# Exchanging the engines of two PSUM evacuations in a windowed-attention loop

## The chip, the cores and the metric

The kernel runs on all 8 cores of one Trainium2 chip. Each core works on its own 2048 of the 16384 tokens and reads all weights; no core waits for another. The metric is the device time of the slowest core, in microseconds. A core has five engines with queues of their own that run in order: TensorE (PE), VectorE (DVE), ScalarE (ACT), GpSimd (POOL) and SyncE (SP). They meet only at semaphores.

## The reference

One transformer layer on x of 2 x 8192 tokens with 1024 features, in 16 heads of 64:

```python
x = x + attn(_layernorm(x), Wq, Wk, Wv, Wo)
x = x + moe(_layernorm(x), gate_w, gate_b, w1, b1, w2, b2)

# attn: windows of 128 tokens, and the sequence's first 64 tokens as global keys
s_g = einsum('bhnqd,bhgd->bhnqg', qw, kg) * scale      # 64 global keys
s_l = einsum('bhnqd,bhnkd->bhnqk', qw, kw) * scale     # 128 keys of the window
attn = softmax(concatenate([s_g, s_l], axis=-1), axis=-1)
out = einsum(attn[..., :g], vg) + einsum(attn[..., g:], vw);  return out @ Wo.T
# moe: all 8 experts, (silu(gh + b) * (xh + b)) @ w2, weighted by a top-2 gate
```

## The kernel before

The program is written by hand: a helper `op(engine, function, waits, inc)` appends to one list per engine, and `runner` (L871) issues each list in order. Before every instruction of ACT or DVE, `runner` also makes the engine wait for its own previous counted instruction (L877). Counters `c_pe`, `c_act`, `c_dve` each stand for one semaphore that is raised by every counted instruction of that engine, so a value of a counter names a place in that engine's list; a wait whose value was already waited for is left out (L880).

Stages, in order: load x and normalize it (LayerNorm by ACT squares and DVE sums); then twice, for each half of 1024 tokens, transpose the normalized tokens, project to q, k, v (`projection`, L302, into PSUM banks pE and pF, evacuated by ACT), and run the attention loop of L519; then the second LayerNorm with the gate; then the experts from L739 on, which are all dense matmuls on PE with weights streamed by POOL's DMA queue.

The change is in the attention loop. A **pair** `pi` is one window (8 per half) with one head (16), so 128 pairs per half. A pair goes through four steps, and the loop at L519 is a software pipeline written out by hand: in **round** j it emits, in this order,

- now and then (j = 22, 38, ...: 8 times per half) `pemit_oproj`, the output projection of a finished window: 2 groups of 8 matmuls of 512 columns, each group added to x by DVE (L506), and then a square-sum of the new x by ACT (L512) and a sum by DVE (L516);
- `pemit_pv(j-6)`: PE multiplies the transposed probabilities `sPT` with the values (L467 for the global keys, L474 for the window) into bank pC or pD, 64 x 128; the result is copied from PSUM to `aof` by DVE (L478);
- `pemit_tr(j-5)`: PE transposes the probabilities `P_sb` in two parts (L447, L452) into pT or pU; they are copied from PSUM to `sPT`, 128 x 256 in bf16, by ACT (L455);
- `pemit_front(j-3)`: ACT takes the exponential of the scores with the row sum as accumulator (L430, two instructions in the trace); DVE takes the reciprocal (L435) and scales the row (L438);
- `pemit_S(j)`: PE computes the scores in two matmuls (L417, L422) into one of three banks pA, pB, pE, after the exponential of pair j-3 has left that bank: `vEXP.get(pi - 3)` in L414.

`sPT` has 2 slots, `P_sb` 4, and pC/pD and pT/pU are each two banks used in turn.

Of the kernel before, what the change touches and what calls it, by code (L numbers as in the profile page):

```python
# [8 lines left out]
BF16 = mybir.dt.bfloat16  # L9
# [4 lines left out]
P = 128  # L14
# [5 lines left out]
HD = 64  # L20
NWIN = 16
GT = 64
# [23 lines left out]
def build_nc(taps=()):  # L46
    nc = bass.Bass("TRN2", target_bir_lowering=False)
# [58 lines left out]
    c_pe = Ctr(sem_pe)  # L106
    c_act = Ctr(sem_act)
    c_dve = Ctr(sem_dve)
# [9 lines left out]
    def op(eng, fn, waits=(), inc=None):  # L118
        streams[eng].append((fn, tuple((c, v) for (c, v) in waits), inc))
        if inc is not None:  # L120
            inc.v += inc.step
        return inc.v if inc is not None else None

    xr = d_x.rearrange("(t p) d -> p t d", p=P)
    for ch in range(4):
        op("sync" if ch % 2 == 0 else "scalar", lambda e, ch=ch: e.dma_start(
            out=x_sb[:, ch * 4:(ch + 1) * 4, :], in_=xr[:, ch * 4:(ch + 1) * 4, :]),
           inc=c_x[ch])
# [76 lines left out]
    def norm_transpose(tt, dst_view, v_extra_waits=(), src=None, parts=P,  # L205
# [30 lines left out]
    es_attn = contextlib.ExitStack()  # L236
# [9 lines left out]
    vgt = es_attn.enter_context(nc.sbuf_tensor("vgt", [GT, D], BF16))  # L246
    gx = es_attn.enter_context(nc.sbuf_tensor("gx", [GT, 8], F32))
    P_sb = es_attn.enter_context(nc.sbuf_tensor("P_sb", [P, 4, 192], BF16))
    sPT = es_attn.enter_context(nc.sbuf_tensor("sPT", [P, 2, 256], BF16))
    rr = es_attn.enter_context(nc.sbuf_tensor("rr", [P, 4, 4], F32))  # L250

    op("sync", lambda e: e.dma_start(out=xg_sb[:], in_=d_xg), inc=c_sy)
# [4 lines left out]
       waits=[(c_sy, v_sync_all[0]), (c_setup, v_gpsetup)], inc=c_dve)  # L257
    op("vector", lambda e: e.tensor_tensor(s_gbl[:], s_gbf[:], s_gbh[:], ALU.subtract),
       inc=c_dve)
# [6 lines left out]
       waits=[(c_sy, v_sync_all[0])], inc=c_act)  # L266
    op("vector", lambda e: e.reduce_sum(gx[:, 0:1], xg_sb[:], axis=AX.X),
       waits=[(c_sy, v_sync_all[0])], inc=c_dve)
    v_gxs = (c_act.v, c_dve.v)
    op("vector", lambda e: e.tensor_scalar_mul(gx[:, 2:3], gx[:, 0:1], 1.0 / D),  # L270
       waits=[(c_act, v_gxs[0])], inc=c_dve)
# [6 lines left out]
       waits=[(c_dve, v_gv)], inc=c_act)  # L278
    op("scalar", lambda e: e.activation(gx[:, 4:5], gx[:, 4:5], AF.Exp, scale=-0.5),
       inc=c_act)  # L280
# [3 lines left out]
       waits=[(c_act, v_grstd)], inc=c_dve)  # L284
# [9 lines left out]
    v_aof_done = [0]  # L294
    v_attn_tail_pe = [0]

    def wproj_load(slot, dram, vfree_pe):
        op("gpsimd", lambda e: e.dma_start(out=wsl[:, slot], in_=dram),
           waits=([(c_pe, vfree_pe)] if vfree_pe else []), inc=c_wsl[slot])
        return (c_wsl[slot], c_wsl[slot].v)  # L300
# [33 lines left out]
    for half in range(2):  # L334
        hbase = half * 8
        v_xn1 = 0
        for t8 in range(8):
            tt = hbase + t8
            waits = [(c_act, v_ln1_rstd), (c_dve, v_ln1_nmr)]
# [14 lines left out]
        if half == 0:  # L354
            for ic in range(DC):
                ps = proj_ps[ic % 2]
                waits = [vwk, (c_act, v_xgn)]
# [3 lines left out]
                for dc in range(DC):  # L361
                    def f(e, ps=ps, dc=dc, ic=ic):
# [5 lines left out]
                       inc=(c_pe if dc == DC - 1 else None))  # L368
# [6 lines left out]
        v_v_act, v_v_pe = projection(vt, 0, vwv, half, 1.0, v_xn1, "tm")  # L375
        if half == 0:
            for tc in range(2):
                ps = proj_ps[tc % 2]
                waits = [vwv, (c_act, v_xgn)]
# [3 lines left out]
                for dc in range(DC):  # L383
                    def f(e, ps=ps, dc=dc, tc=tc):
# [4 lines left out]
                       inc=(c_pe if dc == DC - 1 else None))  # L389
# [3 lines left out]
                   waits=[(c_pe, v_mm)], inc=c_act)  # L393
                v_evac_prev[("proj", tc % 2)] = c_act.v
        vwo = wproj_load(1, d_wot, v_k_pe)
# [6 lines left out]
        vPN = {}  # L402
        vPT = {}
        vPTEV = {}
        vPV = {}
        vAO = {}
# [36 lines left out]
        def pemit_tr(pi):  # L443
            ptb = pT if pi % 2 == 0 else pU

            def ft1(e, ptb=ptb, pi=pi):
                return e.transpose(ptb[0:GT, 0:P], P_sb[:, pi % 4, 0:GT], s_id[:])  # L447
            op("tensor", ft1,
               waits=[(c_dve, vPN[pi]), (c_act, vPTEV.get(pi - 2, 0))], inc=None)

            def ft2(e, ptb=ptb, pi=pi):
                return e.transpose(ptb[:, P:256], P_sb[:, pi % 4, GT:192], s_id[:])  # L452
            op("tensor", ft2, inc=c_pe)
            vPT[pi] = c_pe.v
            op("scalar", lambda e, ptb=ptb, pi=pi: e.copy(  # L455
                sPT[:, pi % 2, :], ptb[:, 0:256]),
               waits=[(c_pe, vPT[pi]), (c_pe, vPV.get(pi - 2, 0))], inc=c_act)
            vPTEV[pi] = c_act.v

        def pemit_pv(pi):  # L460
            w8, head = pi // H, pi % H
            pvb = PV_banks[pi % 2]
            pb = (head % 2) * HD
            ic = head // 2

            def fpv1(e, pvb=pvb, head=head, pi=pi):
                return e.matmul(pvb[0:HD, 0:P], vgt[:, head * HD:(head + 1) * HD],  # L467
                                sPT[0:GT, pi % 2, 0:P], start=True, stop=False)
            op("tensor", fpv1,
               waits=[(c_act, vPTEV[pi]), (c_act, v_v_act),  # L470
                      (c_dve, vAO.get(pi - 2, 0))], inc=None)

            def fpv2(e, pvb=pvb, head=head, w8=w8, pi=pi):
                return e.matmul(pvb[0:HD, 0:P], vt[:, w8, head * HD:(head + 1) * HD],  # L474
                                sPT[:, pi % 2, P:256], start=False, stop=True)
            op("tensor", fpv2, inc=c_pe)
            vPV[pi] = c_pe.v
            op("vector", lambda e, pvb=pvb, pb=pb, ic=ic, w8=w8: e.tensor_copy(  # L478
                aof[pb:pb + HD, ic, w8 * P:(w8 + 1) * P], pvb[0:HD, 0:P]),
               waits=[(c_pe, vPV[pi])], inc=c_dve)  # L480
            vAO[pi] = c_dve.v

        def pemit_oproj(t8):
            v_ao_w = vAO[t8 * H + H - 1]
            for dh in range(2):
                gidx = t8 * 2 + dh
                ps = pF
                waits = [vwo, (c_dve, v_ao_w)]
                pv = v_evac_prev.get("oproj1")
                if pv:  # L490
                    waits.append((c_dve, pv))
                pv2 = v_evac_prev.get(("proj", 1))
                if pv2:
                    waits.append((c_act, pv2))
                for ic in range(DC):
                    def f(e, ps=ps, ic=ic, t8=t8, dh=dh):
                        return e.matmul(ps[:], aof[:, ic, t8 * P:(t8 + 1) * P],  # L497
                                        wsl[:, 1, ic, dh * 512:(dh + 1) * 512],
                                        start=(ic == 0), stop=(ic == DC - 1))
                    op("tensor", f, waits=waits if ic == 0 else [],  # L500
                       inc=(c_pe if ic == DC - 1 else None))
                v_mm = c_pe.v

                def fr(e, ps=ps, t8=t8, dh=dh, hbase=hbase):
                    xs = x_sb[:, hbase + t8, dh * 512:(dh + 1) * 512]
                    return e.tensor_tensor(xs, ps[:], xs, ALU.add)  # L506
                op("vector", fr, waits=[(c_pe, v_mm)], inc=c_dve)
                v_evac_prev["oproj1"] = c_dve.v
                if dh == 1:
                    tt = hbase + t8  # L510
                    v_add = c_dve.v
                    op("scalar", lambda e, tt=tt: e.activation(  # L512
                        lnsq[:, 0:D], x_sb[:, tt, :], AF.Square,
                        accum_out=g_s2[:, tt:tt + 1]),
                       waits=[(c_dve, v_add)], inc=c_act)
                    op("vector", lambda e, tt=tt: e.reduce_sum(  # L516
                        g_s1[:, tt:tt + 1], x_sb[:, tt, :], axis=AX.X), inc=c_dve)

        for j in range(NPAIR + 24):  # L519
# [8 lines left out]
                pemit_front(j - 3)  # L528
            if j < NPAIR:
                pemit_S(j)  # L530
        v_aof_done[0] = c_dve.v

        v_attn_tail_pe[0] = c_pe.v
    v_attn_done_dve = c_dve.v
# [14 lines left out]
       waits=[(c_act, v_st[0])], inc=c_dve)  # L549
# [6 lines left out]
       waits=[(c_dve, v_var)], inc=c_act)  # L556
    op("scalar", lambda e: e.activation(g_rstd[:], g_rstd[:], AF.Exp, scale=-0.5),
       inc=c_act)
# [3 lines left out]
       waits=[(c_act, v_rstd2)], inc=c_dve)  # L562
# [108 lines left out]
    for j in range(NT + 2):  # L671
# [9 lines left out]
       waits=[(c_pe, v_attn_done_pe)], inc=c_setup)  # L681
# [57 lines left out]
    for ei in range(NE):  # L739
        for jfi in range(NJ):  # L740
            for fsl in range(FS_JF):
                fs = jfi * FS_JF + fsl
                slot = (ei * NFS + fs) % W1SLOTS
                for th in range(NTH):
                    par = g1[0] % 2
                    xh, gh = xh_b[par], gh_b[par]
                    waits = [w1_fill_v[(ei, fs)],
                             (c_act, v_ln2_done_act),
                             (c_dve, v_gate_done_dve)]
# [7 lines left out]
                    for hx in range(2):  # L757
                        ps = xh if hx == 0 else gh
                        for dc in range(DC):
                            def f(e, ps=ps, slot=slot, dc=dc, hx=hx, th=th):  # L760
# [5 lines left out]
                               waits=waits if (hx == 0 and dc == 0) else [],  # L766
                               inc=(c_pe if (hx == 1 and dc == DC - 1) else None))
                    v_mm = c_pe.v
                    if th == NTH - 1:
# [5 lines left out]
                       waits=[(c_pe, v_mm), (c_act, v_b1_done)], inc=c_act)  # L775
                    v_a1 = c_act.v

                    def fa2(e, xh=xh, par=par, ei=ei, fs=fs, fsl=fsl, th=th):
# [5 lines left out]
                       inc=c_dve)  # L784
# [3 lines left out]
            for tt in range(NT):  # L788
                for dh in range(2):
                    gq = (tt * 2 + dh) % 2  # L790
                    ps = m2_b[gq]
                    waits = [(c_dve, v_act_ready),
                             (c_dve, v_gate_done_dve),
                             (c_setup, v_b2ld)]
# [6 lines left out]
                    if jfi == 0:  # L801
# [7 lines left out]
                        waits = []  # L809
                    for fsl in range(FS_JF):  # L810
# [3 lines left out]
                        def f(e, ps=ps, fsl=fsl, slot=slot, tt=tt, dh=dh,  # L814
# [6 lines left out]
                           inc=(c_pe if fsl == FS_JF - 1 else None))  # L821
                        first = False
                        waits = []
# [18 lines left out]
    for tt in range(NT):  # L842
        op("sync", lambda e, tt=tt: e.dma_start(
            out=out_r[:, tt, :], in_=x_sb[:, tt, :]),
           waits=[(c_dve, store_after[(tt, 1)])], inc=c_sy)
# [9 lines left out]
    for name in taps:  # L855
        t, dt_, shp = tapmap[name]
        dtap = nc.dram_tensor("tap_" + name, shp, F32, kind="ExternalOutput").ap()
        if dt_ == F32:
            op("sync", lambda e, t=t, dtap=dtap: e.dma_start(out=dtap, in_=t[:]),
               waits=[(c_dve, c_dve.v), (c_act, c_act.v), (c_pe, c_pe.v)], inc=c_sy)  # L860
        else:
            op("gpsimd", lambda e, t=t, dtap=dtap: e.dma_start(out=dtap, in_=t[:]),
               waits=[(c_dve, c_dve.v), (c_act, c_act.v), (c_pe, c_pe.v)], inc=c_setup)
# [77 lines left out]
```

How the kernel before makes its waits and increments, by code:

```python
            def body(eng):  # L872
                marks = {}
                own = own_ctr.get(name)
                n_own = 0
                for fn, waits, inc in streams[name]:
                    if own is not None and n_own > 0:
                        eng.wait_ge(own.sem, n_own)
                    for (ctr, v) in waits:
                        if v > marks.get(ctr.key, 0):
                            eng.wait_ge(ctr.sem, v)
                            marks[ctr.key] = v
                    ins = fn(eng)
                    if inc is not None:
                        assert ins is not None
                        ins.then_inc(inc.sem, inc.step)
                        if inc is own:
                            n_own += 1
```

## Time and profile before

| what | us |
|---|---|
| two plain runs | 6828.25 and 7522.56 |
| their median | 7175.41 |
| the profiled execution, slowest core | 6743.82 |
| its span, first to last instruction (core 2) | 6742.0 |
| spans of the 8 cores in it | 6729.4 to 6742.0 |

The two plain runs are of one program and lie 10% apart, and the profiled execution is lower than either. Durations can be read only from the profiled execution, so everything below is set against its 6743.8 us. Times in the rows are microseconds from the start of the span of core 2 unless they are marked ns. PE is the matmul part of TensorE, PEld its weight loads, which overlap with it. PEclk is the TensorE clock that was granted, as a share of 2.4 GHz: 1.00 is 2.4 GHz and 0.50 is 1.2 GHz.

### The profile page before, as it was taken

What the parts mean: (1) busy time and instruction counts of PE and PEld (TensorE: products, weight loads), DVE (VectorE), ACT (ScalarE), POOL (GpSimd) and SP (SyncE); (2) the same over time, 40 slices, a digit from 0 to 9 for tenths busy, and PEclk for the clock granted to TensorE, in tenths of its full rate; (3) what the DMA queues carried; (4) which work ended last, traced back from release to release, by engine and by line L of the source; (5) the groups of instructions that cost most, each with busy time, mean ns of one, the idle gap of its engine ahead of it and who ended that gap; (6) DMA issues with size and microseconds to landing.
All of it is one profiled execution on the core that took longest, in us unless ns stands there. A gap on an engine that the chain in (4) does not pass through costs nothing.

```text
span 6742.0 us, 77157 instructions; the slowest of 8 cores (6729.4 to 6742.0 us)
## 1 busy us (share of the span) xinstructions
PE 6071.4 (90%) x28296; PEld 2705.8 (40%) x28296; DVE 1859.3 (28%) x3088; ACT 1103.0 (16%) x2056; POOL 278.8 (4%) x530
## 2 busy tenths in 40 slices
PE   4557554999999999999999999999999999999999
PEld 2223223444444444444444444444444444444444
DVE  1231333222222222222222222222222222222222
ACT  3333333111111111111111111111111111111111
POOL 0000000000000000000000000000000000000000
PEclk9657555999999999999999999999999999999999
DMA  4002001122222222222222221222222222221122
GB/s 97 7 1 50 1 1 32 26 36 37 38 38 38 38 38 38 38 38 38 38 35 38 38 38 32 38 38 38 35 35 38 38 35 38 37 36 34 34 35 68
DMA packets 80461, 240.33 MB, mean 36 GB/s; under 512 B 9330, under 2 KB 9346, under 8 KB 79074
## 3 DMA queue, kind: packets, MB, share of 16 engines
q0 software_dynamic: 75312, 218.33, 19.4%
q1 hardware_dynamic: 3730, 12.88, 0.5%
q8 instruction: 238, 3.90, 0.2%
q10 hardware_dynamic: 1056, 4.19, 0.2%
q14 instruction: 125, 1.02, 0.0%
HBM read 445.29 MB, written 8.39 MB: 67 GB/s over the span
## 4 chain that ended last, share of the span: by engine, by line
PE 89%; ACT 5%; issue 2%; DVE 2%; another core or an unknown queue 1%; DMA 0%; ACTq 0%; DVEq 0%; POOLq 0%
PE pE L816 14%; PE pF L816 13%; PE pA L761 13%; PE pB L761 13%; PE pD L761 13%; PE pC L761 13%; ACT P_sb L430 2%; ACT sPT L455 1%; PE pF L497 1%; PE pE L314 1%; PE pF L314 1%; PE pE L803 1%; PE pF L803 1%; PE pD L474 0%
## 5 line engine op out<-in xcount | busy, mean ns | idle before, releaser
L816 PE MATMUL pE<-w2rg,act_sb 128*128 128x512 bf16 x4096 | 999.7, 389 | 65.9 <-DVE act_sb L779 35.1
L761 PE MATMUL pA<-xn2f,w1rg 128*128 128x512 bf16 x4096 | 969.3, 380 | 34.3 <-DVE x_sb L828 31.1
L816 PE MATMUL pF<-w2rg,act_sb 128*128 128x512 bf16 x4096 | 975.9, 382 | 0.0
L761 PE MATMUL pB<-xn2f,w1rg 128*128 128x512 bf16 x4096 | 968.7, 380 | 0.0
L761 PE MATMUL pC<-xn2f,w1rg 128*128 128x512 bf16 x4096 | 967.7, 379 | 0.0
L761 PE MATMUL pD<-xn2f,w1rg 128*128 128x512 bf16 x4096 | 967.7, 379 | 0.0
L772 ACT ACTIVATE a1st<-pB,b1c 128x512 bf16<-128x512 f32 x512 | 351.8, 687 | 3399.4 <-PE pB L761 3399.4
L779 DVE SCALAR_TENSOR_TENSOR act_sb<-pA,b1c,a1st 128x512 bf16<-128x512 f32 x512 | 384.4, 751 | 1465.9 <-ACT a1st L772 1465.9
L779 DVE SCALAR_TENSOR_TENSOR act_sb<-pC,b1c,a1st 128x512 bf16<-128x512 f32 x512 | 384.3, 751 | 1368.8 <-ACT a1st L772 1368.8
L816 PEld LDWEIGHTS pE<-w2rg,act_sb 128*128 128x128 bf16 x4096 | 394.6, 99 | 571.8 <-issue 137.2
L761 PEld LDWEIGHTS pA<-xn2f,w1rg 128*128 128x128 bf16 x4096 | 398.6, 98 | 525.8 <-issue 50.6
L761 PEld LDWEIGHTS pB<-xn2f,w1rg 128*128 128x128 bf16 x4096 | 400.4, 98 | 485.0 <-issue 2.0
L761 PEld LDWEIGHTS pC<-xn2f,w1rg 128*128 128x128 bf16 x4096 | 400.6, 98 | 483.6
L761 PEld LDWEIGHTS pD<-xn2f,w1rg 128*128 128x128 bf16 x4096 | 400.1, 98 | 483.8
L816 PEld LDWEIGHTS pF<-w2rg,act_sb 128*128 128x128 bf16 x4096 | 392.5, 98 | 492.8 <-issue 46.8
L772 ACT ACTIVATE a1st<-pD,b1c 128x512 bf16<-128x512 f32 x512 | 351.8, 687 | 1412.8 <-PE pD L761 1412.8
L828 DVE SCALAR_TENSOR_TENSOR x_sb<-pE,gateW,x_sb 128x512 f32<-128x512 f32 x512 | 384.3, 751 | 653.5 <-PE pE L816 653.5
L828 DVE SCALAR_TENSOR_TENSOR x_sb<-pF,gateW,x_sb 128x512 f32<-128x512 f32 x512 | 384.3, 751 | 557.9 <-PE pF L816 557.9
L704 POOL DMA_DIRECT2D w1rg<-w1r x256 | 135.3, 529 | 3405.5 <-PE pD L761 3337.6
L717 POOL DMA_DIRECT2D w2rg<-w x256 | 135.9, 563 | 1931.8 <-PE pF L816 1931.8
L435 DVE RECIPROCAL rr<-rr 128x1 f32<-128x1 f32 x256 | 41.9, 164 | 461.4 <-ACT P_sb L430 461.4
L417 PE MATMUL pB<-kgf,qf 64*128 64x64 bf16 x86 | 17.8, 207 | 108.9 <-ACT P_sb L430 108.9
(174 smaller groups left out, 1952.4 us busy)
## 6 DMA issues: line engine op xcount, KB each, us to landing
w1rg<-w1r POOLq DMA_DIRECT2D x256, 512.0 KB, 5.0
w2rg<-w POOLq DMA_DIRECT2D x256, 256.0 KB, 9.2
out<-x_sb SPq DMA_DIRECT2D x16, 512.0 KB
x_sb<-x ACTq DMA_DIRECT2D x2, 2048.0 KB, 39.2
x_sb<-x SPq DMA_DIRECT2D x2, 2048.0 KB, 34.7
wsl<-wqt POOLq DMA_DIRECT2D x2, 2048.0 KB, 19.6
wsl<-wkt POOLq DMA_DIRECT2D x2, 2048.0 KB, 32.2
wsl<-wvt POOLq DMA_DIRECT2D x2, 2048.0 KB, 14.9
```

What stands on the lines that cost most here:

```text
L314: return e.matmul(ps[:], wsl[:, wslot, dc, ic * P:(ic + 1) * P], xn1h[:, dc, tc * 512:(tc + 1) * 512], start=(dc == 0), stop=(dc == DC - 1))
L430: op("scalar", lambda e, sb=sb, pi=pi: e.activation(P_sb[:, pi % 4, :], sb[:, 0:192], AF.Exp, bias=s_eps[:, 1:2], accum_out=rr[:, pi % 4, ...
L455: op("scalar", lambda e, ptb=ptb, pi=pi: e.copy(sPT[:, pi % 2, :], ptb[:, 0:256]), waits=[(c_pe, vPT[pi]), (c_pe, vPV.get(pi - 2, 0))], in ...
L497: return e.matmul(ps[:], aof[:, ic, t8 * P:(t8 + 1) * P], wsl[:, 1, ic, dh * 512:(dh + 1) * 512], start=(ic == 0), stop=(ic == DC - 1))
L704: op("gpsimd", lambda e, ei=ei, fs=fs, slot=slot: e.dma_start(out=w1rg[:, slot], in_=d_w1r[ei, fs]), waits=waits, inc=c_w1[slot])
L717: op("gpsimd", lambda e, ei=ei, fs=fs, slot=slot: e.dma_start(out=w2rg[:, slot], in_=d_w2[ei, fs * P:(fs + 1) * P, :]), waits=waits, inc=c ...
L761: return e.matmul(ps[:], w1rg[:, slot, dc, hx, :], xn2f[:, dc, th * 512:(th + 1) * 512], start=(dc == 0), stop=(dc == DC - 1))
L772: op("scalar", lambda e, gh=gh, par=par, ei=ei, fs=fs: e.activation(a1st[:, par, :], gh[:], AF.Silu, bias=b1c[:, ei, NFS + fs:NFS + fs + 1 ...
L779: return e.scalar_tensor_tensor(act_sb[:, fsl, th * 512:(th + 1) * 512], xh[:], b1c[:, ei, fs:fs + 1], a1st[:, par, :], ALU.add, ALU.mult)
L803: return e.matmul(ps[:], s_ones[:], s_b2[:, ei * D + dh * 512: ei * D + (dh + 1) * 512], start=True, stop=False)
L816: return e.matmul(ps[:], act_sb[:, fsl, tt * P:(tt + 1) * P], w2rg[:, slot, dh * 512:(dh + 1) * 512], start=first, stop=fin)
L828: return e.scalar_tensor_tensor(xs, ps[:], gateW[:, tt, ei:ei + 1], xs, ALU.mult, ALU.add)
```

## The change

The two evacuations of a pair exchange engines. The copy of the transposed probabilities PSUM to `sPT` (128 x 256, bf16) goes from ACT to DVE; the copy of the attention output PSUM to `aof` (64 x 128, f32 to bf16) goes from DVE to ACT. Each keeps its place in the program text, and so its place between the other steps of a round in its new engine's list. `sPT` gets 4 slots in place of 2, so the copy into it waits for the PV matmuls of pair pi - 4 and not pi - 2. The waits of PE are turned to the counters of the new engines. The slice `vgt[0:GT, ...]` is all of `vgt`'s partitions, as before.

```diff
-    sPT = es_attn.enter_context(nc.sbuf_tensor("sPT", [P, 2, 256], BF16))
+    sPT = es_attn.enter_context(nc.sbuf_tensor("sPT", [P, 4, 256], BF16))
 def pemit_tr(pi):
             op("tensor", ft1,
-               waits=[(c_dve, vPN[pi]), (c_act, vPTEV.get(pi - 2, 0))], inc=None)
+               waits=[(c_dve, vPN[pi]), (c_dve, vPTEV.get(pi - 2, 0))], inc=None)
...
-            op("scalar", lambda e, ptb=ptb, pi=pi: e.copy(
-                sPT[:, pi % 2, :], ptb[:, 0:256]),
-               waits=[(c_pe, vPT[pi]), (c_pe, vPV.get(pi - 2, 0))], inc=c_act)
-            vPTEV[pi] = c_act.v
+            op("vector", lambda e, ptb=ptb, pi=pi: e.tensor_copy(
+                sPT[:, pi % 4, :], ptb[:, 0:256]),
+               waits=[(c_pe, vPT[pi]), (c_pe, vPV.get(pi - 4, 0))], inc=c_dve)
+            vPTEV[pi] = c_dve.v
 def pemit_pv(pi):
             op("tensor", fpv1,
-               waits=[(c_act, vPTEV[pi]), (c_act, v_v_act),
-                      (c_dve, vAO.get(pi - 2, 0))], inc=None)
+               waits=[(c_dve, vPTEV[pi]), (c_act, v_v_act),
+                      (c_act, vAO.get(pi - 2, 0))], inc=None)
...
-            op("vector", lambda e, pvb=pvb, pb=pb, ic=ic, w8=w8: e.tensor_copy(
+            op("scalar", lambda e, pvb=pvb, pb=pb, ic=ic, w8=w8: e.copy(
                 aof[pb:pb + HD, ic, w8 * P:(w8 + 1) * P], pvb[0:HD, 0:P]),
-               waits=[(c_pe, vPV[pi])], inc=c_dve)
-            vAO[pi] = c_dve.v
+               waits=[(c_pe, vPV[pi])], inc=c_act)
+            vAO[pi] = c_act.v
 def pemit_oproj(t8):
-                waits = [vwo, (c_dve, v_ao_w)]
+                waits = [vwo, (c_act, v_ao_w)]
```

## Rows read from the trace of the kernel before

**Rows 1.** The page: busy time of PE and the granted clock in 40 slices.
```profile
PE 6071.4 (90%) x28296; PEld 2705.8 (40%) x28296; DVE 1859.3 (28%) x3088; ACT 1103.0 (16%) x2056; POOL 278.8 (4%) x530
...
PEclk9657555999999999999999999999999999999999
```

**Rows 2.** Busy time by stage (stretch, length, engines, PEclk, DMA): loops one, two, experts.
```profile
192.70:553.50 360.80, 188.61 (x896) 83.36 (x896) 110.67 (x407) 121.11 (x398) 0.00 (x0) 0.56 0.00 1
...
659.00:1016.00 357.00, 185.17 (x884) 82.19 (x884) 110.65 (x404) 119.95 (x394) 0.56 (x2) 0.56 0.00 1
...
1160.00:6742.00 5582.00, 5458.70 (x24823) 2408.43 (x24821) 1537.23 (x2048) 704.80 (x1025) 263.07 (x498) 0.99 0.22 37
```

**Rows 3.** One line, L417: what ended PE's idle time before it (us, times).
```profile
  ACT P_sb L430: 321.0, 250
```

**Rows 4.** Timeline of one round (start, duration, engine, line, [idle before <-releaser]).
```profile
400.04 0.21 PE L417 MATMUL pB<-kgf,qf 64*128 64x64 bf16 x1 [1.21 <-ACT P_sb L430]
...
400.06 0.29 PE L422 MATMUL pB<-kf,qf 64*128 64x128 bf16 x1
400.26 0.27 DVE L438 TENSOR_SCALAR P_sb<-P_sb,rr 128x192 bf16<-128x192 bf16 x1
...
400.28 0.31 PE L467 MATMUL pC<-sPT,vgt 64*64 64x128 bf16 x1
...
400.52 0.31 PE L474 MATMUL pC<-sPT,vt 128*64 128x128 bf16 x1
...
400.63 0.31 PE L447 MATMUL pU<-s_id,P_sb 128*64 128x128 bf16 x1
...
400.88 0.29 PE L452 MATMUL pU<-s_id,P_sb 128*128 128x128 bf16 x1
400.94 0.28 DVE L478 CAST aof<-pC 64x128 bf16<-64x128 f32 x1 [0.41 <-PE pC L474]
401.25 0.37 ACT L455 COPY sPT<-pU 128x256 bf16<-128x256 bf16 x1 [1.36 <-PE pU L452]
401.72 0.42 ACT L430 ACTIVATE P_sb<-pE,s_eps 128x192 bf16<-128x192 f32 x1
...
402.33 0.16 DVE L435 RECIPROCAL rr<-rr 128x1 f32<-128x1 f32 x1 [1.11 <-ACT P_sb L430]
...
402.38 0.21 PE L417 MATMUL pE<-kgf,qf 64*128 64x64 bf16 x1 [1.21 <-ACT P_sb L430]
```

**Rows 5.** Timeline, the round behind an output projection, PE at full clock.
```profile
289.80 0.19 PE L417 MATMUL pE<-kgf,qf 64*128 64x64 bf16 x1 [2.49 <-ACT P_sb L430]
...
290.14 0.24 PE L474 MATMUL pD<-sPT,vt 128*64 128x128 bf16 x1
...
291.82 0.21 PE L417 MATMUL pA<-kgf,qf 64*128 64x64 bf16 x1 [1.21 <-ACT P_sb L430]
```

**Rows 6.** Groups by form, PSUM evacuations on ACT and DVE (busy us, mean ns | idle before).
```profile
L455 ACT COPY sPT<-pU 128x256 bf16<-128x256 bf16 x128 | 47.7, 372 | 155.5 <-PE pU L452 153.6
...
L327 ACT ACTIVATE kf<-pE 128x512 bf16<-128x512 f32 x16 | 9.6, 597 | 18.1 <-PE pE L314 18.1
...
L370 ACT CAST kgf<-pF 128x64 bf16<-128x64 f32 x4 | 0.8, 212 | 1.1 <-PE pF L363 1.1
...
L478 DVE CAST aof<-pC 64x128 bf16<-64x128 f32 x128 | 36.1, 282 | 48.5 <-PE pC L474 45.8 <-DVE g_s L516 2.4 <-DVE P_sb L438 0.3
...
L506 DVE TENSOR_TENSOR x_sb<-pF,x_sb 128x512 f32<-128x512 f32 x32 | 22.1, 692 | 96.3 <-PE pF L497 96.3
```

**Rows 7.** Short stretches, columns as in rows 2: the loop, then transposes before loop two.
```profile
245.00:250.00 5.00, 2.25 (x12) 1.08 (x12) 1.43 (x6) 2.02 (x8) 0.00 (x0) 0.50 0.00 0
...
555.00:560.00 5.00, 2.90 (x27) 2.31 (x28) 4.04 (x6) 2.70 (x5) 0.00 (x0) 0.73 0.85 138
560.00:565.00 5.00, 3.16 (x39) 2.31 (x37) 2.93 (x4) 4.43 (x5) 0.00 (x0) 0.93 1.01 164
```

More of the change, by code:

```diff
@@ L466, in fpv1 @@
             def fpv1(e, pvb=pvb, head=head, pi=pi):
-                return e.matmul(pvb[0:HD, 0:P], vgt[:, head * HD:(head + 1) * HD],
-                                sPT[0:GT, pi % 2, 0:P], start=True, stop=False)
+                return e.matmul(pvb[0:HD, 0:P], vgt[0:GT, head * HD:(head + 1) * HD],
+                                sPT[0:GT, pi % 4, 0:P], start=True, stop=False)
             op("tensor", fpv1,
-               waits=[(c_act, vPTEV[pi]), (c_act, v_v_act),
-                      (c_dve, vAO.get(pi - 2, 0))], inc=None)
+               waits=[(c_dve, vPTEV[pi]), (c_act, v_v_act),
+                      (c_act, vAO.get(pi - 2, 0))], inc=None)
             def fpv2(e, pvb=pvb, head=head, w8=w8, pi=pi):
                 return e.matmul(pvb[0:HD, 0:P], vt[:, w8, head * HD:(head + 1) * HD],
-                                sPT[:, pi % 2, P:256], start=False, stop=True)
+                                sPT[:, pi % 4, P:256], start=False, stop=True)
             op("tensor", fpv2, inc=c_pe)
             vPV[pi] = c_pe.v
-            op("vector", lambda e, pvb=pvb, pb=pb, ic=ic, w8=w8: e.tensor_copy(
+            op("scalar", lambda e, pvb=pvb, pb=pb, ic=ic, w8=w8: e.copy(
                 aof[pb:pb + HD, ic, w8 * P:(w8 + 1) * P], pvb[0:HD, 0:P]),
-               waits=[(c_pe, vPV[pi])], inc=c_dve)
-            vAO[pi] = c_dve.v
+               waits=[(c_pe, vPV[pi])], inc=c_act)
+            vAO[pi] = c_act.v
         def pemit_oproj(t8):
@@ L530, in build_nc @@
                 pemit_S(j)
-        v_aof_done[0] = c_dve.v
+        v_aof_done[0] = c_act.v
         v_attn_tail_pe[0] = c_pe.v
```

## Prediction

> **What bounds the kernel now.** I read the page first, then busy time by stage, then the waits of PE, and only then the timeline. The page says that PE is busy for 90% of the span and that its granted clock is near full everywhere but in slices 2 to 7 [rows 1]. By stage [rows 2]: the experts take 5582 us, at clock 0.99 and with PE busy for 5459 of them. The diff does not touch them. The two attention loops take 360.8 and 357.0 us; PE is busy for about half of each, at clock 0.56. All that the change can win or lose is in these 718 us.
>
> What does PE wait for there? In front of the first score matmul (L417) it sat idle for 321.0 us in 250 waits, each ended by the exponential on ACT [rows 3]. Of 128 pairs per half the first three need no free bank, so 125 x 2 = 250: every round waits, 1.28 us on average.
>
> The timeline of one round shows the ring that sets its length [rows 4]. Count from the first score matmul, 400.04. PE runs scores, PV and transposes without a break: the second PV matmul is 0.48 to 0.79, the second transpose 0.84 to 1.13. ACT's copy to `sPT` starts at 1.21 (0.08 after the transpose) and ends at 1.58; the exponential starts at 1.68; the next score matmul starts at 2.34, which is 0.66 after the exponential's start. Here the reader should see that the exponential's own scores had been ready for over two rounds. It starts late only because it stands behind ACT's copy in ACT's list, and that copy waits for the transposes, the last thing that PE does in a round. DVE's copy to `aof` starts at 0.90, 0.11 after the PV matmul, and nothing on the ring waits for it. The ring is score, PV, transposes, ACT copy, exponential, score: 2.34 us.
>
> **The change, part by part.**
>
> *ACT.* The instruction ahead of the exponential is now the copy to `aof`, which waits for the PV matmul only. I start it at 0.90, where DVE starts it today (with ACT's lag of 0.08 it would be 0.87). Its price: ACT's casts from PSUM took 212 ns at 64 columns, 372 at 256 and 597 at 512 [rows 6]. From 64 to 256 that is (372 - 212)/192 = 0.83 ns a column, so 128 columns cost 212 + 53 = 265 ns. No row shows 64 partitions or an f32 source at just this width; the bounds are the 212 and the 597 rows, and I take 265 because the operation is nearest to the 64-column cast. The copy ends at 1.165, the exponential starts 0.10 later (the gap of today, 1.58 to 1.68) at 1.265, the next score 0.66 later at 1.925. The round becomes 1.925 us: 0.415 less, of which 0.31 is the earlier start and 0.107 the shorter copy. At the bounds it would be 0.47 less (212) or 0.08 less (597).
>
> The Trainium skill (ScalarE: Activation LUTs, What ACT_TABLE_LOAD costs) gives an ACTIVATE with immediate scale and bias 186 ns plus 0.833 ns an element. By it the copy would be 293 ns, the round 1.95 and the whole sum some 6 us smaller. The slope agrees with the rows, the constant is 27 ns above them (it would give 239 where the cast took 212), so the rows are used.
>
> *DVE.* The copy of 128 x 256 bf16 from PSUM has no row on DVE. The nearest are 282 ns for 128 columns and 692 for 512, f32 from PSUM [rows 6]: (692 - 282)/384 = 1.07 ns a column, so 0.42 us at one column a cycle; below, 0.28, if the type makes it cost no more than the 128-column cast. I take 0.42. Who is behind it? It runs from 1.21 to 1.63. In DVE's list the reciprocal of pair j-3 stands behind it, which cannot start before the exponential is done, at 1.265 + 0.61 = 1.875. The work ahead of it, the scaling, ends at about 0.5. Its reader, the PV matmul of the next round, comes up at 1.925 + 0.24 = 2.165. So it is hidden with 0.43 us to spare with a lag of 0.1. If that cover were gone, a second ring would count (PV, transposes, DVE copy, PV): 1.21 - 0.24 + c + 0.1, or 1.07 + c. It decides from c = 0.86 on.
>
> *PE.* Same matmuls. The transpose's wait on `sPT`'s copy of two pairs before is already covered by the PV wait ahead of it, and PV's bank wait on ACT is covered by the score wait of the round before. Nothing new is queued on PE. Four `sPT` slots cost nothing and remove no wait that shows: a slot's PV was done a full round earlier even with two. No DMA moves; POOL and SP have no work in the loops.
>
> *Sum.* Of the 250 waiting rounds, 14 hold an output projection (7 per half; the eighth comes after the last score) and 4 at the start of the loops have no PV ahead. Of the other 232, I let 14, one behind each projection, run at full clock, since such a round took 2.02 us [rows 5]: its PV matmul ends at 0.58, and the same steps give 0.58 + 0.11 + 0.265 + 0.10 + 0.66 = 1.72, 0.30 less. In the 14 rounds with a projection the ring goes through DVE's add and ACT's square-sum and then the copy, so only the shorter copy counts. Together: 218 x 0.415 + 14 x 0.30 + 14 x 0.107 = 90.5 + 4.2 + 1.5 = 96.2 us. Start and end of the loops, and all stages behind, keep their length. 6743.8 - 96.2 = **6648 us**, a ratio of 0.986. The sum is made against the profiled execution's own 6743.8. The two plain runs, 6828 and 7523, lie 84 and 779 above it with a median of 7175; I forecast for a run like the profiled one, and the 84 us go into the range.
>
> **The rivals.**
>
> *A. As summed*: 6648. Its own range is 6638 to 6724, from the copy at 212 ns (218 x 0.47 + 6 = 108 us) to 597 ns.
>
> *B. PE's clock rises.* In the loop the granted clock is 0.50 [rows 7] with PE busy for 1.13 of 2.34 us, 48%. After the change it is 1.13 of 1.925, 59%. For it: in the transposes ahead of loop two the clock rose from half to full, 0.73 and 0.93 in two stretches of 5 us, though PE had idle gaps [rows 7]. Against it: there PE was busy for 58 and 63% of each stretch partly at full clock already, with 8 transposes back to back, whereas rounds at full clock behind a projection [rows 5] did not keep it; the loop's mean is 0.56 [rows 2]. Rounds of 1.72 in place of 2.34 would give 218 x 0.62 + 6 = 141 us: 6603, and somewhat less if the projections gain too.
> The Trainium skill (TensorE: Matmul & The Clock Gate, The HAM clock gate) says that the gate follows how busy PE has been of late; by that rule a denser loop may be given the full clock, and the time would be B's. The trace agrees in kind, but no row shows at what density between this loop and those transposes it turns.
>
> *C. The copy is not released early.* If ACT saw the PV matmul only when PE has finished the transposes, only the shorter copy and little else would be left: 232 x 0.107 = 25 us, 6719. Against it: DVE is released at 0.90 by the same matmul, before the second transpose ends at 1.13 [rows 4].
>
> *D. DVE becomes the bound, slower than before.* The copy to `sPT` on DVE would have to last. The ring 1.07 + c passes today's 2.34 at c = 1.27 us, and each 0.1 beyond costs 23 us; at 1.5 the kernel takes 6797. Against it: 128 x 512 in f32 with a second operand took 0.69 [rows 6].
>
> **How the numbers follow.** Chances: A 0.78, B 0.12, C 0.07, D 0.03. The predicted time is A's, 6648. The range takes in B at 6603 with some gain at the projections, and on the upper side C and A's value 84 us up, 6732, where the plain run stood above the profiled one: 6590 to 6750. What two measurements of this kernel can tell apart is about 2%, or 135 us. A lies well within, B just beyond. Faster by over 2%: B's 0.12 and 0.06 of A for the scatter that the runs show, 0.18; slower: D's 0.03; the same: 0.79.
>
> **What the profile would show.** A: score matmuls 1.9 us apart; the `aof` copy on ACT near 0.27 us and released by PE L474; the exponential directly behind it; in front of L417 still ACT, but about 0.8 to 0.9 us a round, 225 us in all; `sPT` copies on DVE of 0.28 to 0.42 us with nobody waiting; clock still 0.5; each loop some 48 us shorter; the experts at 5582. B: rounds of 1.7 at clock 1.00. C: the `aof` copies start after 1.13. D: PE waits in front of L467 for DVE. I am wrong if the ACT copy costs much more than its neighbours, if the clock in the loop moves, or if the experts' 5582 us shift by more than the loops gain.

## The result, and the profile after

| what | before | changed |
|---|---|---|
| runs, median | 7093.46 (10 runs, 6745.81 to 7522.56) | 6784.37 (11 runs, 6640.85 to 7522.38) |
| profiled execution | 6743.82 | 6642.19 |
| ratio of undisturbed runs (see below), first measurement | | 0.979, 95% interval 0.969 to 0.989 |
| side by side, undisturbed | 6746.0 to 6750.8 (5 runs) | 6642.5 and 6645.5 |

In 43 of the 66 executions of the two kernels on record, the cores of one die (in at least seven, of both) were granted a lower clock and ended 1 to 17% later, which sets the medians above; "undisturbed" below is a run, or the cores of a die, without it (changed kernel: 6626 to 6644 us). Forecast was 6648, with a range of 6590 to 6750, so the profiled execution missed by 6 us and the median over all runs lies outside the range.

What the profile of the changed kernel shows, first by group (busy us, mean ns | idle before, releaser), to be set beside [rows 6]:

```profile
L455 DVE COPY sPT<-pU 128x256 bf16<-128x256 bf16 x128 | 37.3, 292 | 84.8 <-PE pU L452 82.4 <-DVE g_s L516 2.4
...
L478 ACT CAST aof<-pC 64x128 bf16<-64x128 f32 x128 | 33.3, 260 | 120.2 <-PE pC L474 115.5 <-PE pU L452 2.6
```

The copy to `aof` costs ACT 260 ns and is released by the PV matmul; the copy to `sPT` costs DVE 292 ns. Now the waits in front of L417, then in front of L467 (us, times):

```profile
  ACT P_sb L430: 217.6, 248
...
  DVE sPT L455: 4.3, 8
```

PE still waits for the exponential in nearly every round (248 waits), but for 0.88 us in place of 1.28 [rows 3]; only 8 of 256 PV steps wait for DVE's copy. One round of the timeline (start, duration, engine, line), the counterpart of [rows 4]:

```profile
398.36 0.21 PE L417 MATMUL pE<-kgf,qf 64*128 64x64 bf16 x1 [0.77 <-ACT P_sb L430]
...
398.84 0.31 PE L474 MATMUL pC<-sPT,vt 128*64 128x128 bf16 x1
...
399.19 0.29 PE L452 MATMUL pU<-s_id,P_sb 128*128 128x128 bf16 x1
399.25 0.26 ACT L478 CAST aof<-pC 64x128 bf16<-64x128 f32 x1 [1.03 <-PE pC L474]
399.59 0.29 DVE L455 COPY sPT<-pU 128x256 bf16<-128x256 bf16 x1 [0.73 <-PE pU L452]
399.60 0.42 ACT L430 ACTIVATE P_sb<-pA,s_eps 128x192 bf16<-128x192 f32 x1
...
400.26 0.21 PE L417 MATMUL pA<-kgf,qf 64*128 64x64 bf16 x1 [0.78 <-ACT P_sb L430]
```

From the score matmul: ACT's copy starts at 0.89, the exponential at 1.24, the next score at 1.90. The exponential starts while DVE is still copying the transposed probabilities: ACT's list no longer holds anything that waits for the transposes. By stretch (us, PE, PEld, DVE, ACT, POOL, PEclk, DMA), loop one, five us within it, and the experts:

```profile
192.70:502.70 310.00, 189.98 (x896) 83.67 (x896) 111.79 (x407) 106.67 (x398) 0.00 (x0) 0.56 0.00 1
...
400.00:405.00 5.00, 3.20 (x18) 1.62 (x18) 1.89 (x8) 1.71 (x9) 0.00 (x0) 0.50 0.00 0
...
1060.00:6641.00 5581.00, 5456.81 (x24827) 2410.40 (x24824) 1537.44 (x2048) 705.12 (x1025) 263.10 (x498) 0.99 0.22 37
```

Loop one does the work of [rows 2] in 51 us less, the clock is 0.56 and 0.50 as before, and the same stretch of the experts takes 5581 us for 5582. Of the 102 us gained, 98 are in the two loops.

### The profile page after: what moved, and what is told of

It is laid out like the page before. It is cut to its first block, busy times and chain, and to the rows that moved or that the text cites. A ratio compares the mean times of both kernels' runs of the same rounds, so it can differ in the third digit from the quotient of the medians.

```text
span 6640.4 us, 76935 instructions; the slowest of 8 cores (6631.8 to 6640.4 us)
## 1 busy us (share of the span) xinstructions
PE 6078.0 (92%) x28296; PEld 2711.6 (41%) x28296; DVE 1861.7 (28%) x3088; ACT 1074.4 (16%) x2056; POOL 278.8 (4%) x530
## 4 chain that ended last, share of the span: by engine, by line
PE 90%; ACT 5%; issue 2%; DVE 2%; another core or an unknown queue 1%; DMA 0%; ACTq 0%; DVEq 0%; POOLq 0%
PE pE L816 14%; PE pF L816 14%; PE pA L761 13%; PE pB L761 13%; PE pD L761 13%; PE pC L761 13%; ACT P_sb L430 2%; PE pF L497 1%; ACT aof L478 1%; PE pE L314 1%; PE pF L314 1%; PE pE L803 1%; PE pF L803 1%; PE pD L474 0%
## 5 line engine op out<-in xcount | busy, mean ns | idle before, releaser
L497 PE MATMUL pF<-wsl,aof 128*128 128x512 bf16 x256 | 99.5, 559 | 16.1 <-DVE x_sb L506 15.1
```

The costliest lines, as they stand in the source:

```text
L497: return e.matmul(ps[:], aof[:, ic, t8 * P:(t8 + 1) * P], wsl[:, 1, ic, dh * 512:(dh + 1) * 512], start=(ic == 0), stop=(ic == DC - 1))
```

## The experiments

I call the explanation of the prediction **theory R** (ring): the round is as long as the chain of instructions from one score matmul to the next, and what matters is what stands ahead of the exponential in ACT's list. The rivals say that the load of the engines counts, or the `sPT` slots, or that PE's clock moves.

**e2: only the copy to `sPT` moves to DVE.** The copy to `aof` stays on DVE.

```diff
-            op("scalar", lambda e, pvb=pvb, pb=pb, ic=ic, w8=w8: e.copy(
+            op("vector", lambda e, pvb=pvb, pb=pb, ic=ic, w8=w8: e.tensor_copy(
                 aof[pb:pb + HD, ic, w8 * P:(w8 + 1) * P], pvb[0:HD, 0:P]),
-               waits=[(c_pe, vPV[pi])], inc=c_act)
+               waits=[(c_pe, vPV[pi])], inc=c_dve)
```

> Only half of the change: the copy to sPT goes to DVE, the copy to aof stays on DVE. Theory R (ring): the round is the ring score, PV, copy to aof on ACT, exponential, score; 1.89 us in the changed kernel. With no copy on ACT at all, the exponential stands behind nothing that waits for PE, so that ring is gone. What is left is DVE's own list: the aof copy from 0.90 to 1.18, the sPT copy to 1.57, 0.1 of lag, and PV at 0.24 of the next round: 1.43 us; DVE's four instructions and gaps add up to 1.40. 0.46 us x 218 rounds = 100 us less than the changed kernel: about 6541 (some 6510 if PE's clock rises, since PE would be busy for 1.13 of 1.43). PE idle in front of L417 for the exponential near zero. Rival L (load): what helped was the exchange, each engine getting the copy it does faster; then DVE with both copies is worse than the changed kernel, 6660 to 6740.

Measured: 6570.7 to 6573.3, ratio 0.975 to the kernel before (0.971 to 0.979), 70 us faster than the full change. So the half that moves `sPT` brings more than the whole, and moving `aof` to ACT takes part of it away again. Rival L falls. Of the expected 100 us, 30 are missing. The timeline of e2, DVE's list and PE's PV step, shows why:

```profile
386.20 0.28 DVE L478 CAST aof<-pD 64x128 bf16<-64x128 f32 x1 [0.17 <-DVE P_sb L438]
...
386.66 0.29 DVE L455 COPY sPT<-pT 128x256 bf16<-128x256 bf16 x1 [0.17 <-PE pB L422]
...
387.10 0.28 PE L467 MATMUL pC<-sPT,vgt 64*64 64x128 bf16 x1 [0.51 <-DVE sPT L455]
387.12 0.16 DVE L435 RECIPROCAL rr<-rr 128x1 f32<-128x1 f32 x1 [0.17 <-DVE sPT L455]
...
387.39 0.27 DVE L438 TENSOR_SCALAR P_sb<-P_sb,rr 128x192 bf16<-128x192 bf16 x1
...
387.83 0.28 DVE L478 CAST aof<-pC 64x128 bf16<-64x128 f32 x1 [0.17 <-DVE P_sb L438]
```

From one `aof` cast to the next it is 1.63 us: four instructions of together 1.00 us, and gaps of 0.17, 0.17, 0.11 and 0.17, with DVE never waiting longer than such a gap. I had put all gaps at 0.1. DVE's list is the bound here; that no other order of these four instructions would shorten it was not tried.

**e3: only the copy to `aof` moves to ACT.**

```diff
-            op("vector", lambda e, ptb=ptb, pi=pi: e.tensor_copy(
+            op("scalar", lambda e, ptb=ptb, pi=pi: e.copy(
                 sPT[:, pi % 4, :], ptb[:, 0:256]),
```

> The other half alone: the copy to aof goes to ACT, the copy to sPT stays on ACT (4 slots). Theory R: ACT runs aof 0.89 to 1.15, sPT from 1.24 (ready at 1.21) to 1.61, the exponential at 1.71, the next score 0.65 later: 2.36 us a round, 0.02 above the kernel before: 6748, no change. Rival L (ACT copies 64x128 in 0.26 where DVE took 0.28): some gain, or, if ACT's load counts, 0.35 us x 232 = 81 us slower, 6825.

Measured: 6782.5, 0.5 to 0.6% above the undisturbed runs of the kernel before beside it (6739.4 to 6748.6); one run, so the time alone says little, and the rounds of its trace say more. Timeline of e3:

```profile
395.88 0.21 PE L417 MATMUL pA<-kgf,qf 64*128 64x64 bf16 x1 [1.28 <-ACT P_sb L430]
...
396.77 0.26 ACT L478 CAST aof<-pD 64x128 bf16<-64x128 f32 x1 [1.04 <-PE pD L474]
397.17 0.37 ACT L455 COPY sPT<-pT 128x256 bf16<-128x256 bf16 x1
397.63 0.42 ACT L430 ACTIVATE P_sb<-pB,s_eps 128x192 bf16<-128x192 f32 x1
...
398.29 0.21 PE L417 MATMUL pB<-kgf,qf 64*128 64x64 bf16 x1 [1.28 <-ACT P_sb L430]
```

The round is 2.41 us where 2.36 was expected, since the gap between the two copies is 0.14. An extra 0.26 us copy on ACT costs the round only 0.07, because it runs while ACT would wait for the transposes anyway: load alone is not what counts. Of the 39 us, 0.07 x 218 = 15 are the round. Most of the rest lies in the rounds with an output projection: 12 of the 14 took about 12.0 us here, with every recorded matmul of the projection at half clock, against 3 of 14 over 11.6 before; together they took 165 us for 142. Why the clock rose later was not tried.

**e4: the copy to `aof` released by the transposes.** `pemit_ao` is the copy taken out of `pemit_pv`; it is issued behind `pemit_tr` and waits for `vPT` of its round.

```diff
+            if 0 <= j - 6 < NPAIR:
+                pemit_ao(j - 6, [(c_pe, vPT.get(j - 5, 0))])
```

> The changed kernel, but ACT's copy to aof is made to wait for the transposes of its round. This builds rival C of the prediction. Theory R: the copy starts at 1.21 in place of 0.89, the round is 0.32 longer, 2.21 us: 232 x 0.32 = 74 us more than the changed kernel, 6716. If the early release by the PV matmul is not what brings the gain, it stays at 6642.

Measured: 6727.2 for 6716 expected. Timeline of e4:

```profile
396.17 0.21 PE L417 MATMUL pA<-kgf,qf 64*128 64x64 bf16 x1 [1.10 <-ACT P_sb L430]
...
397.39 0.26 ACT L484 CAST aof<-pC 64x128 bf16<-64x128 f32 x1 [1.36 <-PE pU L452]
...
398.39 0.21 PE L417 MATMUL pB<-kgf,qf 64*128 64x64 bf16 x1 [1.10 <-ACT P_sb L430]
```

Same engines, same instructions, only a later release: the round is 2.22 and 85 of the 102 us are gone. On an average of the eight cores about 74 of them are in the plain rounds, and 12 in those with a projection, where again more matmuls ran at half clock. This is rival C built. It shows that most of the gain is the early release: 0.33 of the 0.445 us a round, the difference between the PV matmul and the end of the transposes.

**e1: two `sPT` slots in place of four.**

```diff
-                sPT[:, pi % 4, :], ptb[:, 0:256]),
-               waits=[(c_pe, vPT[pi]), (c_pe, vPV.get(pi - 4, 0))], inc=c_dve)
+                sPT[:, pi % 2, :], ptb[:, 0:256]),
+               waits=[(c_pe, vPT[pi]), (c_pe, vPV.get(pi - 2, 0))], inc=c_dve)
```

> The changed kernel with 2 slots of sPT in place of 4. Theory R: the PV matmuls of pair pi-2 are done a full round before the copy into their slot, nothing waits: 6642, within 3 us. Rival: the slots carry part of the gain; then waits of the sPT copy on PE appear and the time goes up.

Measured: 6701.9 in one run, in which one die was behind; the cores of the undisturbed die end at 6627.0 to 6640.1, those of the changed kernel's profile at 6632 to 6640, and the loops of one of them take 620 us as there (621). The slots carry nothing of the gain.

**e8: the copy to `aof` twice.** `pemit_ao(j - 6)` is issued twice in a row on ACT.

> The changed kernel with the copy to aof issued twice on ACT (the second writes the same values again). Theory R: that copy lies on the ring, so its 0.26 us and a gap of 0.09 to 0.14 are paid in every round: 232 x 0.37 = 86 us more, 6728. If the copy were hidden, 6642.

Measured: 6741.9 for 6728 expected. Timeline of e8, the two copies merged into one row:

```profile
396.97 0.21 PE L417 MATMUL pE<-kgf,qf 64*128 64x64 bf16 x1 [1.11 <-ACT P_sb L430]
...
397.86 0.60 ACT L484 CAST aof<-pC 64x128 bf16<-64x128 f32 x2 [1.04 <-PE pC L474]
...
399.21 0.21 PE L417 MATMUL pA<-kgf,qf 64*128 64x64 bf16 x1 [1.12 <-ACT P_sb L430]
```

The round is 2.24, 0.345 more than in the changed kernel for 0.34 us of added copy: it is paid in full.

**e9 and e10: the copy to `sPT` twice and four times on DVE.** The `tensor_copy` of L455 is repeated.

> The changed kernel with the copy to sPT issued twice on DVE (same values again). The second ring, PV, transposes, DVE copy, PV, measures 1.14 + c with the lags of the trace of the changed kernel; one more copy with its gap makes c = 0.29 + 0.17 + 0.29 = 0.75 and the ring 1.89, as long as the round is now. Theory R: no change, 6642 within 8 us. If DVE's load as such cost time, 0.46 x 232 = 107 us more.

> The changed kernel with the copy to sPT issued four times on DVE: c = 0.29 + 3 x 0.46 = 1.67, the second ring 1.14 + 1.67 = 2.81 us, 0.92 above the round of now. This builds rival D of the prediction. Theory R: 232 x 0.92 = 213 us more, 6855, slower than the kernel before; PE waits in front of L467 for DVE and no longer in front of L417. If the copy were hidden at any length, 6642.

e9: three runs, 6723.6 to 7697.3, none undisturbed on both dies; the cores of the undisturbed die end at 6633.7 to 6638.0 in the profiled one, with rounds of 1.90, no change from 0.39 us more of DVE's list in each round. e10: 6812.7 in one run, 1% slower than the kernel before; its rounds are 2.58 us. The repeats came 0.39 apart, not 0.46, so c = 0.29 + 3 x 0.39 = 1.46 and the ring 1.12 + 1.46 = 2.58 fits; with 0.39, the 6855 of the expectation would have been 6806. PE's wait in front of the PV step (L476 in e10, us and times) has taken over:

```profile
  DVE sPT L464: 166.2, 242
```

This is rival D built. The same kind of work on the same engine is free up to the point where its ring is the longer one, and paid in full behind it.

**The changed kernel once more, beside the kernel before.** No edit.

> The changed kernel once more, beside runs of the kernel before on the same chip. The profiles say 6743.8 to 6642.2, a ratio of 0.985. The ratio first measured, 0.979 with an interval of 0.969 to 0.989, leans on a plain run of the kernel before at 6828. Theory: with undisturbed runs of both side by side the ratio is 0.985 +- 0.002. Rival: the plain runs gain more than the profiled ones, and it stays at 0.979. All runs taken together, the median is set by how many have a die at a lower granted clock: in each such run the other die's cores should still stand at 6627 to 6642, and the longer die's time should go with its clock alone.

Measured: undisturbed runs 6642.5 and 6645.5 against 6746.0, 6746.7, 6747.0, 6747.7 and 6750.8: 6644/6747 = 0.985. The first ratio of 0.979 had a run of the kernel before at 6828 in it. All eight runs lie between 6642.5 and 7753.9, with a median of 7312.5. The profiled one took 7333.1, with one die at the lower clock. First a core of that die, then one of the other (stretch, length, engines, PEclk, DMA):

```profile
500.00:1000.00 500.00, 307.04 (x1739) 149.63 (x1738) 159.30 (x524) 179.28 (x499) 10.61 (x19) 0.64 0.17 27
...
4000.00:4500.00 500.00, 492.59 (x1840) 196.44 (x1839) 108.82 (x145) 55.76 (x81) 19.02 (x36) 0.81 0.20 30
```

```profile
500.00:1000.00 500.00, 309.44 (x1768) 151.26 (x1769) 157.94 (x523) 179.71 (x499) 9.55 (x17) 0.63 0.15 27
...
4000.00:4500.00 500.00, 488.75 (x2228) 217.53 (x2227) 135.50 (x181) 65.98 (x96) 25.35 (x48) 0.99 0.23 38
```

In the stretch from 500 to 1000 us, most of it in the loops, the two cores do the same work at the same clock. Between 4000 and 4500 us the one is granted 0.81 and gets through 1840 matmuls, the other 0.99 and 2228. So what sets the median over all runs lies, in this execution, in the dense stage that the change does not touch. What lowers the clock was not tried.

**e5: the copy to `aof` a round later in ACT's list.**

```diff
+            if 0 <= j - 7 < NPAIR:
+                pemit_ao(j - 7)
             if 0 <= j - 6 < NPAIR:
                 pemit_pv(j - 6)
```

> The changed kernel, with ACT's copy to aof issued one round later in ACT's list (pair j-7 in place of j-6; the output projections start a round later for it). Theory R: the copy's PV matmul is then done a round before, the exponential stands behind nothing of this round and the first ring is gone. The second ring decides: 1.14 + c with c = 0.29 of the sPT copy, 1.43 us. 218 x 0.46 = 100 us less than the changed kernel, 6541; PE now waits in front of L467 for DVE's sPT copy. Rival: the two copies' load decides and not the order: 6642.

Measured: 6588.4 in one run, with one die behind (6548 to 6587); the other die's cores ended at 6507.8 to 6519.6, where 6541 was expected. PE's PV step in two rounds of a core of that die:

```profile
216.65 0.28 PE L467 MATMUL pD<-sPT,vgt 64*64 64x128 bf16 x1 [0.27 <-DVE sPT L455]
...
218.05 0.28 PE L467 MATMUL pC<-sPT,vgt 64*64 64x128 bf16 x1 [0.27 <-DVE sPT L455]
```

The round is 1.40, and PE waits for DVE's copy: the first ring is gone and the second one is the bound, as the formula says (1.43). The load is the same as in the changed kernel, to the instruction.

**e6: the PV step a round later too.** `pemit_pv(j - 7)`, `pemit_ao(j - 8)`, output projections from j = 24 on. Run twice.

> As e5, and the PV matmuls too one round later (pair j-7, its copy j-8). Theory R: the second ring is gone as well; the round is the longest list: DVE 0.29 + 0.16 + 0.27 with gaps of 0.11 to 0.17 is 1.17, PE 1.12 to 1.2 at half clock, ACT about 1.0. Round 1.2: 218 x 0.69 = 150 us less than the changed kernel, 6492. If PE's clock rises with PE busy for nearly the whole round (rival B of the prediction), DVE still holds the round at 1.17, but output projections run at the full clock: some 20 us less again.

> The kernel of e6 once more, timed in rounds beside the kernel before. Its profile had rounds of 1.17 to 1.18 us, and the cores of the undisturbed die ended at 6448 to 6462. Theory R: an undisturbed run takes 6455 to 6468, 0.957 of the kernel before and 0.972 of the changed kernel. If the shorter loops cost something later in the kernel (the experts' clock), undisturbed runs would come out above 6500.

Measured: in the first, all three runs were disturbed (7169.7 to 7519.4) and the undisturbed die ended at 6448 to 6462; in the second, four of six runs took 6462.3 to 6463.5, ratio 0.9585 to the kernel before (0.956 to 0.961). 30 us less than the 6492 of the expectation, which had left out the rounds behind a projection (1.00 in place of 1.68, 14 times) and those at 1.08 below. DVE's list and two score matmuls in a round of the second, and two stretches of 5 us, in rounds without a projection:

```profile
212.08 0.29 DVE L455 COPY sPT<-pU 128x256 bf16<-128x256 bf16 x1 [0.17 <-DVE P_sb L438]
...
212.49 0.23 PE L417 MATMUL pA<-kgf,qf 64*128 64x64 bf16 x1
...
212.54 0.16 DVE L435 RECIPROCAL rr<-rr 128x1 f32<-128x1 f32 x1 [0.17 <-ACT aof L484]
...
212.81 0.27 DVE L438 TENSOR_SCALAR P_sb<-P_sb,rr 128x192 bf16<-128x192 bf16 x1
...
213.25 0.29 DVE L455 COPY sPT<-pT 128x256 bf16<-128x256 bf16 x1 [0.17 <-DVE P_sb L438]
...
213.66 0.23 PE L417 MATMUL pB<-kgf,qf 64*128 64x64 bf16 x1
```

```profile
205.00:210.00 5.00, 4.77 (x25) 2.42 (x24) 2.88 (x12) 3.01 (x13) 0.00 (x0) 0.50 0.01 2
210.00:215.00 5.00, 5.00 (x27) 2.57 (x27) 3.03 (x14) 2.95 (x12) 0.00 (x0) 0.50 0.01 3
```

The round is 1.17 to 1.18, the sum of DVE's list (0.72 busy and gaps of 0.11 to 0.17). PE is close behind: in 66 of the rounds, those soon after a projection, the score matmuls came 1.08 apart at half clock, with PE busy throughout, while DVE kept to its 1.18. Undisturbed, this version beats both kernels: 4.2% under the one before and 2.7% under the changed one.

**e7: the output projections spread over rounds.** As e6; the two groups of 8 matmuls three rounds apart, DVE's adds one round behind each, ACT's square-sum three rounds behind the second.

> As e6, and each output projection is spread: its two groups of matmuls come three rounds apart, DVE adds each one round later, ACT's square-sum comes three rounds behind. Then PE does not stand between the groups for DVE's add (0.9 us), and ACT's exponentials do not stand behind the square-sum's wait. Expected 3 us less per projection, 14 of them in the loops: about 45 us less than e6, 6445, faster than both kernels: 0.956 of the kernel before. If only PE's own time of the projections counts, it stays at e6.

Measured: 6468.7 in the one undisturbed run of six (the others 7155.6 to 10708.7), and cores of an undisturbed die at 6459 to 6461: not faster than e6. One stretch of six rounds around a projection takes 15.5 us in e7 and 14.8 in e6. Timeline of e7, a second group of matmuls:

```profile
303.91 0.59 PE L501 MATMUL pF<-wsl,aof 128*128 128x512 bf16 x1 [1.10 <-DVE x_sb L511]
```

DVE's add now stands in DVE's list behind a full round's work, and PE waits 1.10 us for it where it waited 0.94 before. The larger part is the clock. All matmuls of the projections by their group, in e6 (second time) and in e7, core 1 of each:

```profile
L503 PE MATMUL pF<-wsl,aof 128*128 128x512 bf16 x256 | 92.9, 529 | 16.1 <-DVE x_sb L512 15.1 <-ACT aof L484 1.0
...
L501 PE MATMUL pF<-wsl,aof 128*128 128x512 bf16 x256 | 106.8, 593 | 18.5 <-DVE x_sb L511 17.5 <-ACT aof L484 1.0
```

Such a matmul is recorded with 0.38 us at full clock and 0.63 at half. On the eight cores of e6, 134 to 184 of the 240 to 256 recorded ones were at half clock; on four cores of e7, 222 to 243. With all sixteen in one round the clock mostly rose on their way; with two groups of eight three rounds apart it seldom did. A group of eight takes 3.57 us at half clock and 1.89 at full, 0.21 a matmul, so some 77 more at half are about 16 us, an estimate. The waits for DVE, 15.1 us that were to go, stayed at 17.5. The two together are some 31 of the expected 45 us; the rest was not taken apart.

## Why the prediction was right or wrong

**The bound and the ring: right.** Every term of the plain round showed up where it was put. The copy was taken as 265 ns and measured 260; it starts at 0.89 for 0.90; the exponential at 1.24 for 1.265; the round is 1.895 for 1.925. e4, e8 and e3 each changed one link of the ring and the round followed by the link's size.

**The cover of DVE's copy: right.** 0.42 us was taken, the lower bound of 0.28 was nearer (292 ns). It was hidden either way: e9 shows no cost with two copies, and e10 confirms the price once the second ring is longer. The point was put at c = 0.86; with the measured lags and round it is about 0.8.

**The sum: right in total, in part by luck.** 96.2 us were forecast, 101.6 came, and errors of both signs stand behind the difference of 5. On core 2, the slowest in both profiles, the rounds without a projection gave 102 in place of 94.7 (218 x 0.445 = 97, and those behind a projection). Another 3 us came at the ends of the loops and 3 outside them, where none were forecast. The rounds with a projection gave 6.4 back where I had put a gain of 1.5. The step "only the shorter copy counts" left out that a projection's length depends on when PE's clock rises within it. Two projections of the changed kernel, two groups of 8 matmuls each:

```profile
265.73 3.60 PE L497 MATMUL pF<-wsl,aof 128*128 128x512 bf16 x8
...
270.27 3.57 PE L497 MATMUL pF<-wsl,aof 128*128 128x512 bf16 x8 [0.94 <-DVE x_sb L506]
...
305.51 3.50 PE L497 MATMUL pF<-wsl,aof 128*128 128x512 bf16 x8
...
309.96 1.89 PE L497 MATMUL pF<-wsl,aof 128*128 128x512 bf16 x8 [0.94 <-DVE x_sb L506]
```

In the first all 16 ran at half clock and the round took 11.55 us, in the second the last 8 ran at full clock and it took 9.77. On core 2 there were 3 long ones of 14 before and 7 after. But the count goes from core to core: 2 to 5 before and 3 to 7 after, and 4 on a core of the second profile of the changed kernel. Over the eight cores the projections took 1.8 us more than before, not 6.4, and the loops together 102.6 us less. That the change itself makes them longer is not shown. On core 2 the weight load for loop two, which waits for the end of loop one, waited 341.4 us in place of 392.2, and its counterpart at the end of loop two 339.0 in place of 386.6: 98 us in the loops.

A slip besides: A's lower end is 6743.8 - 108 = 6636, not 6638.

**Rival B, the clock: fell.** 0.50 in the loop's rounds, as before. **Rivals C and D: fell** for the changed kernel, and were each built as e4 and e10.

**The step that failed** is the last of "How the numbers follow" and of the sum: "I forecast for a run like the profiled one, and the 84 us go into the range". I took the plain run at 6828 as the outer edge of an ordinary scatter, and set aside the one at 7523, though one of the two plain runs shown was there. The table in front said it: two runs of one program 10% apart. A range for the median over all executions had to reach over 6750, since the median before was itself 350 us above the profiled run. The term "84 us up" was the one mis-sized: in the changed kernel's own runs the median stands 142 us above the profiled one and the highest 880, and in the second traced execution a core that ended 697 us late lost 694 of them behind the loops, where its granted clock fell to 0.81. The same step put the 0.18 on faster by over 2%: the ratio came out as 0.979 with an interval that holds 0.98, while side by side it is 0.985, where A had it (0.986). What moved the first ratio was one run of the kernel before.

**What I left unseen**: that half of the change is better than the whole (e2). The prediction said that the exponential stands behind ACT's copy, and then only asked how short the new copy is. It did not ask whether any copy must stand there. With the copy a round later (e5) the same instructions on the same engines take 123 us less (6642 to about 6519, cores of an undisturbed die).

## What to carry to other kernels

In a software pipeline with in-order queues, write down the ring that sets the round: from the waiting instruction back through everything that stands ahead of its producer in the producer's own queue, and what those wait for. Then remove the late wait from that queue, by another engine or, cheaper, by issuing the step one round later; what counts is the longest ring or list, so find the next one before sizing the gain (here 2.34, then 1.90, 1.40 and 1.18). And where plain runs of one program lie 10% apart, forecast the ratio and the undisturbed time, and let the range for the median cover what the runs show.

## What the runs showed of the hardware

- **A PE that the profile calls busy was not always given the full clock.** In e6, stretches with PE busy for 4.77 and 5.00 of 5 us were granted 0.50, that is 1.2 GHz, with matmuls of 64 and 128 columns; experts' matmuls of 512 columns, busy for 98% of their stage, ran at 0.99. In the loops the clock rose only in rounds with a projection, whose matmuls have 512 columns. The profile models the ends of matmuls, so its busy time is not PE at its peak. The Trainium skill (TensorE: Matmul & The Clock Gate, The HAM clock gate) says that the gate goes by how busy the PE has been of late; by the busy share of the profile this did not hold here.
- **A gap on DVE's own list is 0.11 to 0.17 us** with a wait for the own last instruction ahead of each; in e2 four of them are 0.62 of a 1.63 us round.
- **DVE copied 128 x 256 bf16 from PSUM in 292 ns**, nearly what 64 x 128 f32 took (282), for twice the columns. With the 1.07 ns a column of the f32 rows the part without columns is 0.145 us, which leaves 0.57 ns a column for bf16, an estimate. The Trainium skill (VectorE: DVE Perf Modes, Why PSUM operands drop a tier) allows at most twofold speed for 16-bit data from PSUM and none for fp32; the trace agrees.
- **ACT cast 64 x 128 f32 from PSUM in 258 to 260 ns**, 5 to 7 under the line through the 64- and 256-column rows.
